# Edge attributes' part of a graph layer: eight 128-row products a block become twelve 64-row products, placed behind all sixteen transposes

## What is computed

```python
edge_feat = jnp.concatenate([x[src], x[dst], edge_attr], axis=-1)   # 512 + 512 + 64
h = mish(edge_feat @ W1 + b1)
messages = mish(h @ W2 + b2)
agg = jax.ops.segment_sum(messages, dst, num_segments=x.shape[0])
```

## Time and profile before

| what | value |
|---|---|
| median of 3 runs | 1317.8 us (1316.96 to 1317.96) |
| time of the profiled execution | 1319.98 us |
| its span | 1318.3 us |
| TensorE matmul busy | 1244.0 us, 94% of the span |
| VectorE, ScalarE, GpSimd busy | 77%, 65%, 53% |
| mean granted TensorE clock | 0.973 of full speed |

### The profile page before, as it was taken

One profiled execution on the slowest core, in us unless ns is written; L12 is line 12 of the kernel. 1 busy time (PEld: TensorE's weight loads), 2 busy tenths in 40 slices (PEclk: granted clock), 3 DMA queues, 4 the chain that ended last, 5 costly groups with the idle time before them and its releaser, 6 DMA issues. The chain is left out here.

```text
span 1318.3 us, 18957 instructions
## 1 busy us (share of the span) xinstructions
PE 1244.0 (94%) x5844; PEld 997.8 (76%) x5844; DVE 1014.9 (77%) x1799; ACT 851.6 (65%) x772; POOL 697.9 (53%) x482
## 2 busy tenths in 40 slices
PE   7986999999999999999999999987799997999998
PEld 5764777777777777787777777776587776888886
DVE  3425799999999999999999999854776247757444
ACT  2306999999999999999999999746532001212210
POOL 0036888888888888888888888243320000011000
PEclk8897999999999999999999999988899997999999
DMA  9997877777778777777778777796200610000001
GB/s 288 316 333 161 170 141 148 148 154 157 152 156 160 159 146 144 150 152 155 155 154 160 160 146 137 203 345 249 80 2 0 220 65 0 17 1 2 0 25 56
DMA packets 107195, 183.59 MB, mean 139 GB/s; under 512 B 34994, under 2 KB 44512, under 8 KB 106872
## 3 DMA queue, kind: packets, MB, share of 16 engines
q0 software_dynamic: 70704, 105.14, 41.0%
q1 hardware_dynamic: 29336, 65.40, 14.4%
q10 hardware_dynamic: 7088, 12.20, 2.9%
HBM read 141.21 MB, written 41.30 MB: 138 GB/s over the span
## 5 line engine op out<-in xcount | busy, mean ns | idle before, releaser
L228 POOL DMA_INDIRECT w_raw<-q_dram,idx_all x172 | 362.6, 2108 | 75.5 <-issue 57.7
L1062 PE MATMUL ps_x<-wA_hi,hT_hi 128*128 128x512 f32 x668 | 270.8, 405 | 1.3 <-DVE hT_lo L753 1.3
L1062 PE MATMUL ps_x<-wA_hi,hT_lo 128*128 128x512 f32 x668 | 264.0, 395 | 0.0
L1062 PE MATMUL ps_x<-wA_lo,hT_hi 128*128 128x512 f32 x668 | 263.6, 395 | 0.0
L228 POOL DMA_INDIRECT w_raw<-p_dram,idx_all x176 | 181.9, 1034 | 114.8 <-DMA q_dram<-x 61.7
L1062 PEld LDWEIGHTS ps_x<-wA_hi,hT_hi 128*128 128x128 f32 x668 | 125.4, 188 | 34.2 <-issue 1.7
L1062 PEld LDWEIGHTS ps_x<-wA_hi,hT_lo 128*128 128x128 f32 x668 | 125.2, 187 | 30.9
L1062 PEld LDWEIGHTS ps_x<-wA_lo,hT_hi 128*128 128x128 f32 x668 | 125.2, 187 | 28.5
L762 DVE TENSOR_TENSOR x<-ps_x,b 128x512 f32<-128x512 f32 x167 | 113.6, 681 | 27.4 <-PE ps_x L1062 27.4
L1736 POOL TENSOR_TENSOR tmp_n<-X,gam 128x512 f32<-128x512 f32 x10 | 13.9, 1393 | 224.7 <-DVE t_be L1821 180.1
L1021 PE MATMUL ps_x<-ident,w_raw 128*128 128x128 f32 x672 | 103.0, 277 | 17.9 <-issue 10.1
(11 more groups left out here) (268 smaller groups left out, 2857.0 us busy)
## 6 DMA issues: line engine op xcount, KB each, us to landing
ea_raw<-in_eaT SPq DMA_DIRECT2D x88, 128.0 KB, 4.6
adj_dram<-adj_sb POOLq DMA_DIRECT2D x42, 210.2 KB, 9.9
adj_dram<-agg_sb ACTq DMA_DIRECT2D x11, 640.5 KB, 11.2
U_lo<-adj_dram SPq DMA_DIRECT2D x10, 640.0 KB, 8.5
adjT_dram<-adjT_sb SPq DMA_DIRECT2D x10, 640.0 KB, 7.7
adjT_rest<-adjT_dram SPq DMA_DIRECT2D x7, 640.0 KB, 9.5
w_raw_g<-in_w SPq DMA_DIRECT2D x4, 1024.0 KB, 7.6
agg_dram<-agg_sb POOLq DMA_DIRECT2D x42, 84.0 KB, 3.4
```

The lines of the kernel that those rows point to most:

```text
L228: g.indirect_dma_start(G[:, slot, c * D:(c + 1) * D], None, rows, bass.IndirectOffsetOnAxis(ap=idx_all[:, i:i + 1], axis=0), **op).then_in ...
L1062: last = t.matmul(ps_x2[c % 2][:, :], h[:, b.slot, e], w[:, k, :], start=(k == 0 and i == 0), stop=(k == KD - 1 and i == 2))
```

## The change

TensorE's `first` becomes one function for the whole block. It turns all sixteen tiles first, and then makes the attributes' products in groups of two chunks: for each of three terms (high\*high, low\*high, high\*low) one product over partitions 0 to 63 into one chunk's bank, and one over partitions 64 to 127 into the next chunk's bank. That is twelve products over 64 rows in place of eight over 128 rows, and the low\*low term is no longer made. `ea_parts` now holds the high part in both halves, in one slot; a new tile `ea_low` holds the low part in both halves. The split is made one step later (block s+2 instead of s+3), and its wait is for the first layer of the block just before instead of two before. `pre_ready` gets its four counts at once.

```diff
-            ea_parts = sb("ea_parts", [P, 2, BE], F32R, edges)
+            ea_parts, ea_low = sb("ea_parts", [P, BE], F32R, edges), sb("ea_low", [P, BE], F32R, edges)
...
                 if b.real():
                     dve_.wait_ge(ea_in[b.slot], b.slot_count(32))
-                    if b.at(-2).real():
-                        dve_.wait_ge(pre_ready, b.at(-2).count(KD))
-                    v.tensor_copy(ea_parts[:, b.slot, :], ea_raw[:, b.slot, :]).then_inc(ea_hi, 1)
+                    if b.at(-1).real():
+                        dve_.wait_ge(pre_ready, b.at(-1).count(KD))
+                    v.tensor_copy(ea_parts[:, :], ea_raw[:, b.slot, :]).then_inc(ea_hi, 1)
                     dve_.wait_ge(ea_hi, b.count(1))
-                    v.tensor_tensor(ea_parts[ED:P, b.slot, :], ea_raw[ED:P, b.slot, :],
-                                    ea_parts[ED:P, b.slot, :].bitcast(F32), ALU.subtract).then_inc(ea_ready, 1)
+                    v.tensor_tensor(ea_low[:, :], ea_raw[:, b.slot, :],
+                                    ea_parts[:, :].bitcast(F32), ALU.subtract).then_inc(ea_ready, 1)
...
-                split_edge_attr(s.at(3))
+                split_edge_attr(s.at(2))
...
-            def first(b, f):
+            def first(b):
...
                 if b.real():
-                    if f == 0:
-                        pe.wait_ge(q_in[b.slot], b.slot_count(16 * TE))
-                    if f % 2 == 0 and b.at(-1).real():
-                        pe.wait_ge(h1_ready, b.at(-1).count(2, f // 2 + 1))
-                    out = ps_x1[:, f * BE:(f + 1) * BE]
-                    for c in range(TE):
-                        t.matmul(out[:, c * P:(c + 1) * P], G[:, b.slot, c * D + f * P:c * D + (f + 1) * P], ident[:, :],
-                                 start=(c == 0), stop=False, is_transpose=True)
-                    if f == 0:
-                        pe.wait_ge(ea_ready, b.count(1))
-                    for i, w in enumerate((wc_hi, wc_lo)):
-                        last = t.matmul(out, w[:, f * P:(f + 1) * P], ea_parts[:, b.slot, :], start=False, stop=(i == 1))
-                    last.then_inc(pre_ready, 1)
+                    pe.wait_ge(q_in[b.slot], b.slot_count(16 * TE))
+                    for f in range(KD):
+                        if f % 2 == 0 and b.at(-1).real():
+                            pe.wait_ge(h1_ready, b.at(-1).count(2, f // 2 + 1))
+                        for c in range(TE):
+                            t.matmul(ps_x1[:, f * BE + c * P:f * BE + (c + 1) * P], G[:, b.slot, c * D + f * P:c * D + (f + 1) * P],
+                                     ident[:, :], start=(c == 0), stop=False, is_transpose=True)
+                    pe.wait_ge(ea_ready, b.count(1))
+                    for f0 in range(0, KD, 2):
+                        for i, (w, part) in enumerate(((wc_hi, ea_parts), (wc_hi, ea_low), (wc_lo, ea_parts))):
+                            for f, rows in ((f0, slice(0, ED)), (f0 + 1, slice(ED, P))):
+                                last = t.matmul(ps_x1[:, cols(f, BE)], w[rows, cols(f, P)], part[rows, :], start=False, stop=(i == 2))
+                    last.then_inc(pre_ready, KD)
...
-                for f in range(KD):
-                    first(s.at(1), f)
+                first(s.at(1))
                 second(s, 0)
```

More of the change, by code:

```diff
@@ L209, in gnn @@
                        h1, Y, w_raw, b3, wA_hi, wA_lo, w3_hi, w3_lo, wc_hi, wc_lo, b2, agg_sb, p_dram, q_dram, agg_dram, adj_dram, eaT, xT_dram,
-                       w03, w04, w3b_in, w4_in, zero_out, zero_agg, p_in, q_in, ea_raw, ea_in, x2, z0_out, z0_dram, z_in, ea_parts, oh_src, adj_summed, agg_summed)
+                       w03, w04, w3b_in, w4_in, zero_out, zero_agg, p_in, q_in, ea_raw, ea_in, x2, z0_out, z0_dram, z_in, ea_parts, ea_low, oh_src, adj_summed, agg_summed)
         U_lo, U_hi = sb("U_lo", [P, R * D], F32R), sb("U_hi", [P, R * D], F32R)
@@ L551, in edge_phase @@
                h1, Z, w_raw, b3, w2_hi, w2_lo, w3_hi, w3_lo, wc_hi, wc_lo, b2, agg_sb, p_dram, q_dram, agg_dram, adj_dram, eaT, xT_dram,
-               w03, w04, w3b_in, w4_in, zero_out, zero_agg, p_in, q_in, ea_raw, ea_in, x2, z0_out, z0_dram, z_in, ea_parts, oh_src, adj_summed, agg_summed):
+               w03, w04, w3b_in, w4_in, zero_out, zero_agg, p_in, q_in, ea_raw, ea_in, x2, z0_out, z0_dram, z_in, ea_parts, ea_low, oh_src, adj_summed, agg_summed):
     HB = 2 * BE
```

## The result

The changed kernel ran in 1314.95 us (median of 18) beside 1318.14 us for the kernel before, 3.2 us less by the medians. The ratio of the runs is 0.9968, 95% interval 0.9958 to 0.9978: 4.2 us faster (2.9 to 5.5). In a second series, with fresh runs of both, it was 0.9968 again (0.9955 to 0.9981). Every ratio in this document leaves out the executions that took far longer than the others of their kernel: one of these 18, at 2477.91 us, and further down one of five and two of six of the two kernels with four pairs. The profiled execution had a span of 1312.1 us.

The account below looks back on a forecast made before the run. TensorE, never running dry in the edge blocks (17.44 us period), was taken as the bound. Per block 0.467 - 0.33 = 0.14 us, times 41 is 5.7 us, so 1317.8 becomes 1312 us; range 1298 to 1330.

Parts of the forecast that it names:

- Faster, by side by side products: First layer on TensorE: two products in different halves stream at the same time, net 0.14 us saved a block; chance 0.56.
- the rival's price: First layer: the two products of a pair go one after another, 1.27 us more a block, 1370 us; chance 0.12.
- Six places cost 1.40 us, and loads keep up: Attributes' products: six pairs at 0.234 us, 0.467 less than before; two weight loads a pair, 0.22 us, just fit.
- Transposes together are worth nothing: First layer: sixteen transposes cost 16 x 0.110 = 1.76 us before and after, so grouping them saves nothing.
- 0.33 us for the changes of shape: TensorE going from 128 rows to 64 and back once a block costs 0.33 us, half a pair's skew included.
- the 42-row reading: Small transposes in the preparation, the trace's one such shape change, leave 0.25 to 0.45 us for entering and leaving.
- the prediction's first rival, no change: Entering, leaving and a pair's skew cost 0.41 to 0.53 us; time within 2.6 us of 1317.8; chance 0.17.
- "Whatever TensorE saves" up to 0.51 us counts: VectorE waits 0.51 us a period for TensorE's second layer; only TensorE savings beyond that would be lost.
- Block 0 free, 41 blocks alike: Edge blocks: block 0's first layer is hidden because block 1 waits for gathered rows, so 41 of 42 count.
- The sum: Edge blocks: 41 x 0.14 = 5.7 us saved, taking the median from 1317.8 to 1312 us.
- the forecast of at least 2.6 us: Whole kernel: faster by 2.6 us up to 19.1 us, 1298.7 to 1315 us; chance 0.56.
- The split, its wait and the queues cost nothing: VectorE's split keeps its lengths, the copy's new wait is met 0.92 us ahead, and nothing changes on a queue.

Follow-up runs that it names:

- four pairs: Changed kernel without the high times low weight term, four pairs instead of six: 1310.7 us; also with VectorE's second `message_low` ahead of the third `x2_of`: 1300.4 us.
- all on one half: Changed kernel with all twelve products reading partitions 0 to 63, so no two use different halves: 1370.2 us (one run).
- order-only kernel: Changed kernel's order (sixteen transposes first, split one step later) with the old eight products over 128 rows: 1319.38 us beside 1320.28, ratio 0.9988.
- the swap: VectorE's second `message_low` put ahead of the third `x2_of`: in the changed kernel 1314.48 us, ratio 0.9951; in the kernel before, ratio 0.9993.
- three and three: Changed kernel with three products over partitions 0 to 63, then three over 64 to 127, for each two chunks: 1315.6 us (one run).

## Why the prediction was right, and where it wasn't

- **Faster, by side by side products.** Right. Pairs follow at 0.23 us, and all on one half gives 18.69 us a period and 1370.2 us, as the rival's price said (17.43 + 1.27 = 18.70, 1370). Against the order-only kernel, the pairs and their two changes of shape take 3.61 - 3.53 = 0.08 us off a first layer, which is the 0.467 less the 0.39.
- **Six places cost 1.40 us, and loads keep up.** Right. At 514.71 the loads for the next pair start with the running pair, for the same halves. By the Trainium skill, TensorE: Matmul & The Clock Gate, Part 3, The mechanism, a load runs beside a product only over other rows. The loads at 514.71 disagree, and the measurement decides; the same section also lets a load into the background weight buffer go ahead, which would fit them.
- **Transposes together are worth nothing.** Nearly right: about 0.02 us a block, 0.6 to 0.7 us in all, by the order-only kernel.
- **0.33 us for the changes of shape.** The mechanism was right, the size too small: 0.20 in and 0.20 out, in sum 0.39, where the 42-row reading had given 0.25 to 0.45 for both. That is 0.02 us short of the 0.41 from which the prediction's first rival, no change, would have begun. The Trainium skill's rule in TensorEngine Tiling (Array Packing), Key Properties, that a change of tiling mode drains TensorE, is borne out in kind: no load ran ahead over either change. The cost was half the length of a product and not the whole. Net saving 17.43 - 17.33 = 0.10 us a block where VectorE is in time, 0.02 of it by the order, and not 0.14.
- **"Whatever TensorE saves" up to 0.51 us counts.** This step failed in its mechanism. VectorE's idle 0.51 us was no free room. It lies behind TensorE's last product, while the work that TensorE waits for lies ahead of it. From VectorE's wait at L763 over its 17.0 us of work to the low part, and from there to `sums`, a chain returns to TensorE after two blocks. With six pairs it took 0.03 us a block in the first profile of the changed kernel (17.35 against 17.32 with the swap) and 0.09 in the second (17.42), and with four pairs about half of what TensorE saved. The prediction had VectorE wait 0.37 us a period for the second layer; it waited 0.45 (14.9 us in 580):

```profile
DVE x L763 <- PE ps_x L1064: 14.9, 35, 0.9
```

- **Block 0 free, 41 blocks alike.** Not quite, but nothing that the change did: block 1 took 0.6 us more than before in one pair of profiles and the same in the other.
- **The sum.** 5.7 us predicted; 4.2 us measured (2.9 to 5.5; 3.2 by the medians of the first series); 2.5 and 1.7 us in the edge blocks of the two pairs of profiles. With the terms as the traces have them, the sum is 41 x (0.08 + 0.02 - 0.03) = 2.9 us with the low part as it was in the first profile, and about 0.4 us with it as in the second. By the traces alone, the forecast of at least 2.6 us would have held narrowly or not at all; the measured 4.2 lies above what they explain. One to three microseconds stay open, and that the total came near 5.7 is partly luck.
- **The split, its wait and the queues cost nothing.** Right for the split and its wait, see 517.15 and 517.60 above. No run here separates the queues.

## What to carry to other kernels

A product over half of the array's rows cost as much as a whole one here (0.23 us); only a partner in the other half makes it pay. The visit to half-array products cost 0.39 us, nearly two products at their pace of 0.23, so gather everything that can use it behind one change of shape: one visit a block was faster than the old form, two were slower. Idle time on the second-busiest engine is not room to spare unless it stands before the work that the bound engine waits for; look where in the chain the wait is, not how long. Such a chain also lets one engine's lateness through to the other, so it costs more in some executions than in others (0.03 and 0.09 us a block). Moving that work ahead of an independent instruction (the swap) gave the steadiest periods and the lowest ratio here with the full computation, 0.9951 against 0.9968, though these two intervals overlap.

## What the hardware showed that I had not expected

TensorE's two halves behaved as two queues. A product of the other half started ahead of two earlier ones (three and three: mean period 17.36 against 17.35 us), and with six ahead of it, once about four were left. So the exact alternation in the source wasn't needed, only that the partner stands within some three or four products; each of the two orders was profiled once. No weight load ran ahead over a change of shape, though loads ran ahead inside each group and, in the order-only kernel, from transposes to products over the same 128 rows. And the cost of the change depends on what follows: about 0.15 us when leaving for transposes, 0.20 us for 512-column products.
